# One scan per state over both channel halves in a mixture-of-experts and state-space kernel

## What is computed

```python
x = x + 0.5 * ffn(layernorm(x))
x = x + attn(layernorm(x))
x = x + 0.5 * ffn(layernorm(x))
```

```python
dA = exp(dt[..., None] * A)
dBx = (dt * xc)[..., None] * Bm[:, :, None, :]
h = dA_t * h + dBx_t
y = einsum('bdn,bn->bd', h, C_t)
```

## Time and profile before

| what | value |
|---|---|
| median of 3 runs | 1273.47 us (1270.12 to 1273.81) |
| profiled execution: its own time, that is, the span from the first to the last instruction | 1272.6 us |
| TensorE, matmuls (PE) | 1253.2 us, 98% |
| VectorE (DVE) | 1114.1 us, 88% |
| ScalarE (ACT) | 926.6 us, 73% |
| GpSimd (POOL) | 394.3 us, 31% |
| mean granted TensorE clock | 0.998 |

### The profile page before, as it was taken

The page is one execution under the profiler, slowest core; times in us unless marked ns, Lnnn a source line. Parts: engine busy times, 40 slices in busy tenths (PEclk is TensorE's granted clock), DMA queues, the critical chain, the costliest instruction groups (busy, mean ns, idle before and its releaser), DMA issues.

```text
span 1272.6 us, 21027 instructions
## 1 busy us (share of the span) xinstructions
PE 1253.2 (98%) x7584; PEld 1096.0 (86%) x7584; DVE 1114.1 (88%) x1481; ACT 926.6 (73%) x1778; POOL 394.3 (31%) x459
## 2 busy tenths in 40 slices
PE   7999999999999999999999999999999999999998
PEld 5888888888888888888888888888888888888887
DVE  4544899989999999999999999999999989999433
ACT  5645978978886978877968788798867968654421
POOL 0101333334342423343333433333334333332110
PEclk9999999999999999999999999999999999999999
DMA  8211677777788868787987878887978887895111
GB/s 244 52 26 30 146 155 154 147 154 158 152 180 164 170 132 183 159 165 161 180 177 150 166 164 176 158 168 148 186 157 167 163 165 142 163 183 107 35 33 33
DMA packets 109303, 182.96 MB, mean 144 GB/s; under 512 B 11024, under 2 KB 23824, under 8 KB 109200
## 3 DMA queue, kind: packets, MB, share of 16 engines
q0 software_dynamic: 56336, 102.79, 45.9%
q1 hardware_dynamic: 52864, 78.85, 24.7%
HBM read 76.22 MB, written 2.62 MB: 62 GB/s over the span
## 4 chain that ended last, share of the span: by engine, by line
PE 73%; DVE 8%; DMA 8%; issue 5%; ACT 3%; POOL 2%; SPq 0%; DVEq 0%; POOLq 0%; ACTq 0%
PE PS L700 27%; PE PS L643 14%; PE PS L646 14%; PE PS L644 14%; DMA Y<-HS 5%; DVE HB L825 2%; DVE HS L923 2%; DMA XS<-DX 2%; DVE HS L931 1%; PE PS L730 1%; PE PS L715 1%; DVE HS L912 1%; PE PS L658 1%; POOL Y L1137 1%; DVE YE L818 1%
## 5 line engine op out<-in xcount | busy, mean ns | idle before, releaser
L700 PEld LDWEIGHTS PS<-WD,HB 128*128 128x128 f32 x4096 | 536.6, 191 | 44.0 <-issue 1.5
L700 PE MATMUL PS<-WD,HB 128*128 128x128 f32 x4096 | 540.1, 275 | 0.0
L1016 ACT ACTIVATE HB<-PS 128x512 f32<-128x512 f32 x512 | 294.3, 596 | 272.9 <-PE PS L646 270.8
L825 DVE TENSOR_TENSOR HB<-PS,HB 128x512 f32<-128x512 f32 x512 | 348.7, 682 | 119.2 <-PE PS L646 110.9
L1137 POOL DMA_DIRECT2D Y<-HS x252 | 221.1, 972 | 383.7 <-DVE HS L931 262.7
L1120 POOL DMA_DIRECT2D XT<-YE x126 | 117.9, 936 | 433.2 <-DVE YE L818 407.4
L643 PE MATMUL PS<-XH,WG 128*128 128x512 f32 x512 | 244.5, 478 | 3.3 <-ACT XH L996 2.3
L643 PE MATMUL PS<-XH,WU 128*128 128x512 f32 x512 | 204.9, 400 | 0.0
L646 PE MATMUL PS<-XH,WG 128*128 128x512 f32 x512 | 203.2, 397 | 0.6 <-DVE XH L883 0.6
L646 PE MATMUL PS<-XH,WU 128*128 128x512 f32 x512 | 202.1, 395 | 0.0
L644 PE MATMUL PS<-XH,WG 128*128 128x512 f32 x512 | 201.0, 393 | 0.0
(11 more groups left out here) (109 smaller groups left out, 1080.9 us busy)
## 6 DMA issues: line engine op xcount, KB each, us to landing
BCB<-BCD SPq DMA_DIRECT2D x128, 512.0 KB, 5.3
Y<-HS POOLq DMA_DIRECT2D x252, 256.0 KB, 6.4
XT<-YE POOLq DMA_DIRECT2D x126, 256.0 KB, 4.4
XS<-DX POOLq DMA_DIRECT2D x7, 512.0 KB, 9.2
XT<-in_L_attn_x_dram SPq DMA_DIRECT2D x8, 256.0 KB, 6.5
WD<-in_L_ffn_w_down_dram SPq DMA_DIRECT2D x8, 256.0 KB, 4.8
out_dram<-XT SPq DMA_DIRECT2D x8, 256.0 KB, 5.6
HS<-in_L_ffn_w_gate_dram SPq DMA_DIRECT2D x6, 256.0 KB, 4.0
```

Source lines behind the costliest of these rows:

```text
L700: z = pe.matmul(expert(g)[:, j, :], HB[:, i % NH, j * P:(j + 1) * P], WD[:, e, c, :], start=c == 0 and j == 0, stop=c == FC - 1 and j == S ...
L825: v.tensor_tensor(H, up(i), H, ALU.mult).then_inc(S["v_h"], 1)
L1016: a.activation(HB[:, i % NH, :], gate(i), ACT.Silu).then_inc(S["a_sil"], 1)
```

## The change

The two scans of a state become one. DA, DX and HS get 8 columns (GAP) behind each half, and the scan runs over the row of both halves with the gap between them. In the gap the decay is 1 in the first column and 0 in the seven others, and the input is 0 (DX is 0 there, so that `s_b`, which in even tiles is now 520 columns wide per half, writes zeros). So the first column keeps the last state of half 0 for `s_car`, the others clear the state, and half 1 begins from zero. In odd tiles, half 0 begins from `car` as before; for half 1, ScalarE copies its carry into the last column of the gap behind the decays of the state (one more activation per state, and `a_da` is raised behind it). The scan has 1033 columns in even tiles and 1032 in odd ones, in place of two of 513 or two of 512. `v_sc` now counts one per state. The planned costs become 2.36 for a scan and 1.44 in place of 1.24 for the decays of a state in odd tiles, and `scans` yields once per state where it yielded twice. One memset is added at the start.

```diff
--- before.py
+++ after.py
@@ -48,6 +48,7 @@
 LATEST = 0.2
 SIGNAL = {"pe": .14, "v": .12, "a": .15, "p": .1}
 BURST = 2
+GAP = 8
 
 
 def timetable():
@@ -238,7 +239,7 @@
         m = decayed[0]
         if m < NT * NS and m // NS in dt_at and m + BURST <= done[0] + NA and (must or (
                 dt_at[m // NS] < clock["pe"] + .5 and clock["a"] < clock["pe"] + CALM)):
-            at = step("s_da", m, after=dt_at[m // NS], a=2.56 + 1.24 * BURST)
+            at = step("s_da", m, after=dt_at[m // NS], a=2.56 + (1.24 if m // NS % 2 == 0 else 1.44) * BURST)
             for k in range(BURST):
                 decay_at[m + k] = at
             decayed[0] = m + BURST
@@ -265,9 +266,8 @@
             m = t * NS + n
             if decayed[0] <= m:
                 decays(must=True)
-            for j in range(2):
-                at = step("s_scan", t, n, j, after=decay_at[m], v=1.22)
-                yield True
+            at = step("s_scan", t, n, after=decay_at[m], v=2.36)
+            yield True
             done[0] = m + 1
             decays()
             while t not in begun_y:
@@ -489,9 +489,9 @@
         HT = sb("HT", [P, 2, 3])
         SZ = sb("SZ", [P, 2, 2, T])
         Y = sb("Y", [P, 2, 2, T])
-        DX = sb("DX", [P, 2, 2, T + 1])
-        DA = sb("DA", [P, NA, 2, T + 1])
-        HS = sb("HS", [P, HR, 2, T + 8])
+        DX = sb("DX", [P, 2, 2, T + GAP])
+        DA = sb("DA", [P, NA, 2, T + GAP])
+        HS = sb("HS", [P, HR, 2, T + GAP])
         car = sb("car", [P, 2, NS])
         PS = ctx.enter_context(nc.psum_tensor("PS", [P, 8, T], F32))
         ident = CON[:, 0:P]
@@ -736,7 +736,8 @@
             wt = Waits(v)
             v.memset(mhalf[:, :], -0.5).then_inc(S["init"], 1)
             v.memset(DA[:, :, :, T], 1.0).then_inc(S["init"], 1)
-            v.memset(DX[:, :, :, T], 0.0).then_inc(S["init"], 1)
+            v.memset(DA[:, :, :, T + 1:T + GAP], 0.0).then_inc(S["init"], 1)
+            v.memset(DX[:, :, :, T:T + GAP], 0.0).then_inc(S["init"], 1)
             dv = 0
 
             def own(z):
@@ -907,26 +908,27 @@
                             wt.wait_ge(S[f"c_y{j}"], 16 * (m - HR + 1))
                     if m >= HR and (m - HR) // NS % 2 == 0:
                         wt.wait_ge(S["a_car"], carried(m - HR))
-                    w = T + 1 if t % 2 == 0 else T
+                    w = T + GAP if t % 2 == 0 else T
                     rows = BCB[:, m % BR, :, :].rearrange("p k l -> p (k l)")[:, 0:w]
                     v.tensor_tensor(HS[:, m % HR, :, 0:w], rows.unsqueeze(1).broadcast_to([P, 2, w]), DX[:, t % 2, :, 0:w],
                                     ALU.mult).then_inc(S["v_db"], 1)
                 elif k == "s_scan":
-                    _, t, n, j = s
+                    _, t, n = s
                     m = t * NS + n
                     wt.wait_ge(S["v_db"], m + 1)
                     wt.wait_ge(S["a_da"], m + 1)
                     if t % 2:
                         wt.wait_ge(S["a_car"], carried(m - NS))
-                    w = T + 1 if t % 2 == 0 else T
-                    H = HS[:, m % HR, j, 0:w]
-                    v.tensor_tensor_scan(H, DA[:, m % NA, j, 0:w], H, car[:, j, n:n + 1] if t % 2 else 0.0,
+                    w = T + GAP + (T + 1 if t % 2 == 0 else T)
+                    H = HS[:, m % HR, :, :].rearrange("p j l -> p (j l)")[:, 0:w]
+                    D = DA[:, m % NA, :, :].rearrange("p j l -> p (j l)")[:, 0:w]
+                    v.tensor_tensor_scan(H, D, H, car[:, 0, n:n + 1] if t % 2 else 0.0,
                                          ALU.mult, ALU.add).then_inc(S["v_sc"], 1)
                 elif k == "s_hc":
                     _, t, n = s
                     m = t * NS + n
                     H = HS[:, m % HR, :, 0:T]
-                    wt.wait_ge(S["v_sc"], 2 * m + 2)
+                    wt.wait_ge(S["v_sc"], m + 1)
                     wt.wait_ge(S[f"c_bc{m % BR}"], 16 * (m // BR + 1))
                     v.tensor_tensor(H, BCB[:, m % BR, 1, :].unsqueeze(1).broadcast_to([P, 2, T]), H, ALU.mult).then_inc(S["v_hc"], 1)
                 elif k == "s_yz":
@@ -1080,14 +1082,17 @@
                         else:
                             wt.wait_ge(S["v_dt"], 1)
                         if m >= NA:
-                            wt.wait_ge(S["v_sc"], 2 * (m - NA + 1))
+                            wt.wait_ge(S["v_sc"], m - NA + 1)
                         for j in range(2):
                             z = a.activation(DA[:, m % NA, j, 0:T], XS[:, t % 2, j, 3:3 + T], ACT.Exp, scale=aneg[:, j, n:n + 1])
+                        if t % 2:
+                            wt.wait_ge(S["a_car"], carried(m - NS))
+                            z = a.activation(HS[:, m % HR, 0, T + GAP - 1:T + GAP], car[:, 1, n:n + 1], ACT.Copy)
                         z.then_inc(S["a_da"], 1)
                 elif k == "s_car":
                     _, t, n = s
                     m = t * NS + n
-                    wt.wait_ge(S["v_sc"], 2 * m + 2)
+                    wt.wait_ge(S["v_sc"], m + 1)
                     a.activation(car[:, :, n], HS[:, m % HR, :, T], ACT.Copy).then_inc(S["a_car"], 1)
 
         @block.gpsimd
@@ -1097,12 +1102,12 @@
                 k = s[0]
                 if k == "ln_first":
                     wt.wait_ge(S["v_ve"], 1)
-                    wt.wait_ge(S["init"], 3)
+                    wt.wait_ge(S["init"], 4)
                     gp.tensor_tensor(rs[:, :], ve[:, :], mhalf[:, :], ALU.pow).then_inc(S["p_rs"], 1)
                 elif k == "ln_square":
                     _, q, b = s
                     wt.wait_ge(S["a_sq"], q)
-                    wt.wait_ge(S["init"], 3)
+                    wt.wait_ge(S["init"], 4)
                     gp.tensor_scalar(ve[:, :], squares[:, :], 1.0 / P, EPS_LN, ALU.mult, ALU.add).then_inc(S["p_ve"], 1)
                     wt.wait_ge(S["p_ve"], q)
                     gp.tensor_tensor(rs[:, :], ve[:, :], mhalf[:, :], ALU.pow).then_inc(S["p_rs"], 1)
```

## The result

The changed kernel took 1281.36 us (median of 6 runs), the kernel before 1273.07 us (median of 6 runs on the same chip). The ratio is 1.0065 with a 95% interval of 1.0049 to 1.008: slower by 0.65%, outside the predicted range and on the side that had a chance of 0.22.

The account below looks back on a forecast made before the run. TensorE was taken as the bound, VectorE nearly filling its shadow. 1272.6 - 3.7 (tail) + 2.0 (late multiplies) + 0 (order) = 1270.9, or 1271.8 us as median, no change that can be told; own range 1270 to 1276, all cases 1266.5 to 1278.5.

Parts of the forecast that it names:

- The saving on VectorE: Scans on VectorE: 2.22 us even and 2.28 odd, start to start; VectorE relieved of 10.5 us.
- The tail, -3.7: Last norm and router, 1184.53 to 1193.94 us: x sooner ends TensorE's waits and clock fall; 3.7 us saved, ends 0 and 3.9.
- this sum would come before 1173 us: End of the last scan stage: the last sum into x, at 1178.78 us before, would come before 1173 us.
- Late multiplies, +2.0: Expert slots: multiplies behind the whole scan come up to 1.2 us later and hold the up matmul; 2.0 us lost.
- The upper end of 7.6: Late expert multiplies at worst: some 22% of 128 scans late by 0.27 us on average, 7.6 us; lower end 0.9.
- The order written anew: 0, with 4.0 both ways: TensorE in 138 to 1184 us: new planned costs shift later steps; its 4.0 us of waits may go or double.
- the signs of being wrong: Over 6 us of new TensorE waits on L825, scans above 2.4 us, or a clock fall in the middle.
- No transfer is added; the additions into Y come at most 0.1 us sooner: Transfers: none added, and additions into Y at most 0.1 us sooner; no cost entered in the sum.
- GpSimd at nothing: GpSimd (pool): named in a heading, with no line on its instructions and no cost in the sum.
- ScalarE at nothing: ScalarE: 64 carry copies of 200 ns, 12.8 us in odd tiles, costed at nothing, at most 0.2 us once or twice.
- Late multiplies win: Rival, chance 0.22, slower: scans ahead of expert multiplies hold up matmuls; 1277.4 us, or 1279.4 with lower clock.
- The merge saves no VectorE time: Rival, chance 0.06, no change: a long scan costs more than its elements, the last norm stays late; 1275.5 us.

Follow-up runs that it names:

- e1: The changed kernel run once more with no edit, to get a trace of ordinary length: 1280.15 us, 1.0068.
- e3: Kernel before, its order kept on every engine, with the merged scan and its copy where the first half scan stood: 1275.77 us, 1.0038.
- e2: Changed kernel's order, but each scan step runs the two old scans back to back, without gap or copy: 1280.47 us, 1.0073.
- e8: Kernel before, two scans in two steps, only planned costs altered (1.18 a half scan, 1.44 for odd decays): 1279.64 us, 1.005.
- e17: Changed kernel with SyncE holding tile 7's first B and C loads until tile 6's additions into Y have landed: 1276.33 us, 1.0037.
- e14: Changed kernel's order with two scans back to back, three small GpSimd operations left out of every norm but the first: 1279.08 us, 1.0055.
- e13: Changed kernel with the three small GpSimd operations of every norm but the first left out: 1277.0 us, 1.0034.
- e4: Kernel before, its order kept, with the merged scan where the second half scan stood: 1280.38 us, 1.006.
- e5: Changed kernel with tile 6's last product, projection and sum into x moved some three expert slots later: 1277.06 us, 1.0037.
- e15: Changed kernel with eight steps moved later, among them closings of tiles 6 and 4 and norm 19's transposes: 1276.32 us, 1.0035.

## Why the prediction was wrong, step by step

**The saving on VectorE: right.** Scans of 2.30 and 2.36 us, 298 us in all; from the start of a scan to the start of the next operation it is 2.22 us in even tiles (671.54 to 673.76 us of e1) and 2.28 in odd ones (837.78 to 840.06 of e3), as worked out. VectorE is busy 1102.3 us in place of 1114.1.

**The tail, -3.7: right in size, wrong in its cause.** No wait and no fall of the clock in 1184 to 1196 us. But e3, merged in the old order, still waits 1.0 and 0.7 us there, and e2, with two scans, doesn't. So the gain came with the order, not from time saved. A new order does not bring it by itself: e8 waits 1.0 and 0.7 us there too. In e1 the transposes simply stand later, 9.1 us behind the last sum into x (1185.10 and 1194.23 us), where it was 7.8 us before. The claim that this sum would come before 1173 us was wrong; it came 6.3 us later than before. The last product of tile 6 did end 7 us sooner (1036.1 against 1043.3 us), but dx of tile 7 comes at 1062.7 us against 1051.0; in e17, where the closing isn't late, it still comes at 1058.4, so most of that is the order as well. And the clock's share of the 3.7 was not tied to those waits: in e3 and e8 the same two waits are followed by a clock of 1.00.

**Late multiplies, +2.0: right.** HB<-L826 costs 1.6 us, 3 times, longest 0.7; in e2, whose two scans stand back to back as one block, 2.0, and in e8, whose halves can be parted, nothing. The upper end of 7.6 was far off.

**"The order written anew: 0, with 4.0 both ways": the step that failed.** The waits are 11.1 us in place of 4.0; less 1.6 for the multiplies, 5.5 more, and 3.0 us of clock behind the longest: +8.5, beyond the bound of 4.0. With it and the 1.6 the sum is 1272.6 - 3.7 + 1.6 + 8.5 = 1279.0, against a span of 1279.9. I bounded the unknown by the waits that the kernel before happened to have. That was no bound: a new order can come out worse by more than all of them. e2, e8 and e14 bear it out (+6.9 to +8.9 us with no merge at all). I had also priced the clock at 2 us a time only under the rival of the multiplies, and nowhere for a wait of the order. A fall of the clock in the middle stood among the signs of being wrong, and it came.

**"No transfer is added; the additions into Y come at most 0.1 us sooner": wrong.** None was added, but one was moved beside another: three loads of tile 7 left 0.4 us ahead of the last addition of tile 6, which then took 10.8 us. e17 undoes that alone and gives back 3.8 us. It accounts for that place only: e17 is still 4.8 us behind the kernel before. Of a transfer it is not enough to count how many there are; what leaves beside it matters.

**GpSimd at nothing: wrong.** The heading named the pool and no line was written on its instructions. A small GpSimd operation that starts while VectorE is in a scan was held to the scan's end, and a merged scan held one nearly 2 us (e3). In the old order that goes with 2.1 of the 4.2 us that the merge costs; in the new one with about 0.7 (e1 and e13), less than the intervals tell apart.

**ScalarE at nothing: borne out.** The 64 copies took 186 ns each, and none of the waits of e1 names a decay or a copy.

**The rivals.** *Late multiplies win* has the sign and comes near the size (1277.4 to 1279.4) but not the mechanism, so the 0.22 was on the right side for another reason. *The merge saves no VectorE time* is excluded by the scans. None of the rivals was "the order comes out worse", though e8 shows that it needs no more than two numbers in the planner. What stays open: why this order puts tile 6's end where it does, and why the merge in the old order loses 8.9 us in e4. e5, e15 and e17 mend single places and stay 4.2 to 4.8 us behind the kernel before, at waits that shift with every edit; I did not find an order in which the merge wins, and can't exclude one.

## What to carry to other kernels

Where the order of a kernel is written from planned costs, an edit of one cost is an edit of the whole order: price it by running the new costs with the old instructions, and take the spread of such runs, not today's waits, as the range. Time saved on an engine that runs in another's shadow is worth only the waits that it ends, and a longer uncuttable instruction on VectorE can also lengthen the smallest operation of GpSimd beside it. When a transfer on the critical path is late, look first at what another queue issued in the microsecond before it.

## What the runs showed of the hardware that was not expected

- The last addition of 256 KB into Y of tile 6 landed after 10.6 to 11.3 us where three loads of 512 KB had left 0.2 to 0.4 us before it (e1, e2, e5, e13, e14), and after at most 4.9 us with these loads held (e17).
- A GpSimd operation on 128x4 took 0.19 us alone and 2.16 us beside a scan of VectorE, ending with it to 0.01 us; another took 2.92 us in place of 1.04, ending 0.84 us behind the scan in which it started. That second one is at 671.76 us of e1, GpSimd and then VectorE in order of time:

```profile
671.76 2.92 POOL L1113 TENSOR_TENSOR rs<-ve,mhalf 128x4 f32<-128x4 f32 x1
```

```profile
671.54 2.30 DVE L925 TENSOR_TENSOR_SCAN HS<-DA,HS 128x1033 f32<-128x1033 f32 x1
```

- Which GpSimd operation is held is not only a matter of which starts first. Before the change the middle one (rs) ran its usual 1.04 us from 418.04 us though a scan started at 418.42, and that scan took its usual 1.22 us; the first one (ve), started at 549.39 us, was held to 550.89 by a scan that started at 549.64.
- A single wait of TensorE of 3.3 us was followed in e1 by a granted clock of 0.50 (the lower level) over 1052 to 1056 us and cost 3.0 us more by it. In e14 a wait of 3.0 us at the same place was followed by 1.00.
